# A gated delta rule over 2048 tokens: projections, norms and gates made beside the spike membranes and kept in DRAM, scaled keys moved from GpSimd to VectorE

## What is computed

```python
h = silu(causal_conv(rms(x)))                       # (2048, 128)
q, k, v = heads(h @ Wq), heads(h @ Wk), heads(h @ Wv)   # 8 heads x 64
q = q / (norm(q) + 1e-6);  k = k / (norm(k) + 1e-6)
drive = heads(h @ Wspike)
alpha_base = heads(silu(h @ Wau + bau) @ Wad + bad)
beta_base = h @ Wbeta + bbeta

def step(carry, ins):                               # over 2048 tokens
    s, mem = carry
    mem = 0.9 * mem + dt
    spike = (mem > 0.5)
    mem = mem - spike * 0.5
    alpha = sigmoid(at + asp * spike)
    beta = sigmoid(bt + sum(spike * bsp))
    active = sum(abs(spike)) > 0
    alpha = where(active, alpha, 1);  beta = beta * active
    s = s * alpha
    s = s + (beta * kt) * (vt - kt @ s)
    return (s, mem), qt @ s
```

## Time and profile before

| | us |
|---|---|
| median of 3 runs | 1695.24 (1692.81 to 1695.54) |
| profiled execution, its own time | 1701.06 |
| its span | 1699.3 |
| TensorE busy, weight loads | 1178.4, 902.6 |
| VectorE, ScalarE, GpSimd busy | 1103.5, 601.2, 198.3 |
| mean granted TensorE clock | 0.795 of full |

### The profile page before, as it was taken

One profiled execution on the slowest core, in us unless ns is written; L12 is line 12 of the kernel. 1 busy time (PEld: TensorE's weight loads), 2 busy tenths in 40 slices (PEclk: granted clock), 3 DMA queues, 4 the chain that ended last, 5 costly groups with the idle time before them and its releaser, 6 DMA issues. The chain is left out here.

```text
span 1699.3 us, 25028 instructions
## 1 busy us (share of the span) xinstructions
PE 1178.4 (69%) x8364; PEld 902.6 (53%) x8364; DVE 1103.5 (65%) x3471; ACT 601.2 (35%) x935; POOL 198.3 (12%) x189
## 2 busy tenths in 40 slices
PE   1230001488888988898888988889666879688786
PEld 1110001377777877787777876779423526346272
DVE  4788988777887778877797777872133325343251
ACT  3120000333444334443444534441325355363422
POOL 2000001301211012110211102110010102001000
PEclk8575555688899889898988999895578788886966
DMA  2000000000000000000000000000200000000000
GB/s 72 0 1 1 1 1 1 1 1 0 0 0 0 0 0 0 0 0 0 0 0 0 0 0 0 0 1 1 58 0 1 0 0 8 0 7 1 0 8 6
DMA packets 9746, 7.22 MB, mean 4 GB/s; under 512 B 3158, under 2 KB 7831, under 8 KB 9690
## 3 DMA queue, kind: packets, MB, share of 16 engines
q1 hardware_dynamic: 8170, 5.07, 1.1%
q10 hardware_dynamic: 1520, 1.48, 0.3%
HBM read 5.50 MB, written 1.05 MB: 4 GB/s over the span
## 5 line engine op out<-in xcount | busy, mean ns | idle before, releaser
L1133 DVE TENSOR_TENSOR delta_tm<-delta_tm,ps 128x256 f32<-128x256 f32 x96 | 40.4, 421 | 156.7 <-PE ps L836 156.7
L795 PE MATMUL ps<-delta_kq_up,delta_arena 64*128 64x128 f32 x1024 | 111.2, 400 | 37.2 <-ACT delta_kq L547 36.5
L795 PEld LDWEIGHTS ps<-delta_kq_up,delta_arena 64*128 64x128 f32 x1024 | 102.4, 302 | 62.2 <-ACT delta_kq L547 37.4
L893 PE MATMUL ps<-ones,beta_b 1*128 1x1 f32 x8 | 1.8, 346 | 190.9 <-PEq L339 190.9
L633 ACT ACTIVATE delta_xf<-ps 128x256 f32<-128x256 f32 (+1 forms) x128 | 48.9, 382 | 204.5 <-PE ps L823 140.2
L517 POOL TENSOR_TENSOR delta_km<-delta_beta_k,delta_arena 128x512 f32<-128x512 f32 x16 | 32.6, 2037 | 635.9 <-DVE delta_beta_k L1030 635.9
L834 PE MATMUL ps<-delta_xf,delta_tt 128*128 128x64 f32 x768 | 106.6, 284 | 0.0
L836 PE MATMUL ps<-delta_tt,delta_xf 128*128 128x64 f32 x768 | 106.6, 284 | 0.0
L823 PEld LDWEIGHTS ps<-delta_tm,drive 128*128 128x128 f32 x768 | 95.6, 201 | 17.0 <-DVE delta_zb L984 9.1
L893 PEld LDWEIGHTS ps<-ones,beta_b 1*128 1x128 f32 x8 | 1.8, 322 | 191.1 <-issue 191.1
L823 PE MATMUL ps<-delta_tm,drive 128*128 128x64 f32 x768 | 98.5, 284 | 6.1 <-ACT delta_tm L623 6.1
(11 more groups left out here) (372 smaller groups left out, 2923.1 us busy)
## 6 DMA issues: line engine op xcount, KB each, us to landing
out<-post_rows SPq DMA_DIRECT2D x4, 256.0 KB, 2.3
setup_wmod<-in_L_wmod ACTq DMA_DIRECT2D x2, 384.0 KB, 3.4
post_wff<-in_L_attn_Wff SPq DMA_DIRECT2D x3, 256.0 KB
post_w<-in_L_ffn_w SPq DMA_DIRECT2D x2, 256.0 KB
post_fc_q<-in_L_ffn_fc_q SPq DMA_DIRECT2D x2, 256.0 KB
setup_wspike<-in_L_attn_Wspike ACTq DMA_DIRECT2D x1, 256.0 KB
wq<-in_L_attn_Wq ACTq DMA_DIRECT2D x1, 256.0 KB
wk<-in_L_attn_Wk SPq DMA_DIRECT2D x1, 256.0 KB
```

The source lines that it names most:

```text
L795: ins = eng.matmul(m.ps[:, at + h % 2, P * (h // 2):P * (h // 2) + P], up_lift[s][ks, cs], m.kq_up[s][ks, :, half], start=True, stop=True)
L1133: eng.tensor_tensor(v, v, m.ps[:, 6 + n, 0:256].rearrange("p (b s) -> p b s", s=s), ALU.subtract).then_inc(vector_back, vec.one(f"TX{x}{s}"))
```

## The change

- A function `prepare()` is added to the block of the membranes. In 4 groups of 512 tokens it makes k, q, v, the gate's hidden units (by ScalarE's Silu, with a change of table before and behind), its drive with `wad`, beta's scores from the tokens, sums of squares and norms. TensorE has 7 steps of 4 matmuls of 512 columns in each group, ScalarE 16 to 19 activations, mostly of 128x2048. VectorE multiplies k and q by the inverse norms (`unit`, one 128x2048 multiplication), 8 times in all, put into the membranes' steps 80, 122, 164 and so on. SP stores 5 MB for each group (20 MB in all), and the phase ends when the last store has landed.
- The three passes of the membranes are written out, without the hardware loop. `WARM` is 128, so each pass still has all its 128 steps.
- In `delta_phase` SP loads for each chunk `zb` (512 KB), `kq` (512 KB) and `v` (256 KB). Each load waits until the chunk before has used the tile.
- GpSimd only clears `drive` at the start. Its `km` operations go to VectorE, its product of spikes and their weights becomes four scalar_tensor_tensor that add into `zb`, its squares are gone.
- TensorE loses k, q, v, the hidden units, `wad`, the sums and half of beta's matmuls. The count moves from behind the first join to before `transposed`.
- VectorE loses the hidden units, the guard of the norms and the multiplication by the norms. Each join is split in its halves a and b, with pieces of the front between; the scaled keys are made before `update` where half of `kq_up` was made behind it. ScalarE loses the norms and the copies of k, q, v, and the lifts come earlier.

VectorE's loop, and what TensorE's chunk loses, as a diff:

```diff
             with eng.Fori(0, NT - 1) as i:
                 front_spikes(i + 1)
                 base(i)
-                front_au(i + 1)
                 blocks(i)
                 front_z(i + 1)
                 front_sums(i + 1)
-                join(i, 8)
                 front_active(i + 1)
-                join(i, 16)
-                front_exponents(i + 1)
-                join(i, 32)
-                front_exponents2(i + 1)
+                join(i, 8, "a")
+                join(i, 8, "b")
+                front_decay(i + 1)
+                join(i, 16, "a")
+                front_mid(i + 1)
+                front_splits(i + 1, UPPER[:1])
+                join(i, 16, "b")
+                front_splits(i + 1, UPPER[1:])
+                front_toend(i + 1)
+                join(i, 32, "a")
+                front_beta(i + 1)
+                join(i, 32, "b")
+                front_base(i + 1)
+                front_upper(i + 1, UPPER[:1])
                 rest(i)
-                front_unit(i + 1)
+                front_upper(i + 1, UPPER[1:3])
                 keep(i)
-                front_upper(i + 1, UPPER[:2])
+                front_upper(i + 1, UPPER[3:])
                 update(i)
-                front_upper(i + 1, UPPER[2:])
                 front_late(i + 1)
...
-            def chunk(i, last):
+            def chunk(i):
 
                 base(i)
                 eng.wait_ge(scalar_back, act.before("out", i))
-                front_au(i + 1)
-                blocks(i, True)
-                front_sums(i + 1)
+                blocks(i)
+                front_beta(i + 1)
+                front_count(i + 1)
                 transposed(i)
                 join(i, 8)
-                front_count(i + 1)
                 join(i, 16)
                 join(i, 32)
...
                 last_join(i)
                 state1(i)
                 solve(i)
-                front_late(i + 1)
                 seen_by_q(i)
-                if not last:
-                    eng.wait_ge(scalar_back, act.at("kend", i))
-                    front_k(i + 2)
                 eng.wait_ge(scalar_back, act.at("solved", i))
-                if not last:
-                    front_q(i + 2)
                 state2(i)
```

More of the change, by code:

```diff
@@ L348, in spike_phase, with a_pass @@
         a_half, b_half = slice(0, W), slice(W, 2 * W)
[L349 to L365, removed]
+        unit, n_units = prepare(nc, ctx, m, block)
+        FIRST, EVERY = 80, 42
         @block.vector
         def _(eng):
-            def a_pass():
+            def a_pass(at=None, t0=0):
                 eng.sem_clear(step_a)
@@ L402, in changed @@
                 return value
-            with eng.Fori(0, SURE) as _:
-                a_pass()
+            for n in range(SURE):
+                a_pass(n * P, 0 if n else P - WARM)
             with eng.If(changed() > 0):
@@ L526, in _ @@
             eng.wait_ge(m.chain_v, 2)
-            front(0)
-            with eng.Fori(0, NT - 1) as i:
-                front(i + 1)
         @block.scalar
@@ L713, in head, with front_beta @@
                 return slice(HD * (h % 2), HD * (h % 2) + HD), slice(P * (h // 2), P * (h // 2) + P)
-            def project(bank, w, rhs, rows=P):
+            def front_beta(n):
+                eng.wait_ge(vector_front, fvec.at("spikes", n))
+                eng.wait_ge(vector_back, vec.before("up8b", n))
                 for c in range(NP):
-                    ins = eng.matmul(m.ps[:, bank, c * P:c * P + P], w[:, c * P:c * P + P], rhs, start=True, stop=True)
-                return ins
-            def front_k(n):
-                project(4, m.wk, m.hh[:, tok(n)]).then_inc(tensor_front, fpe.one("k"))
@@ L996, in front_z, with front_decay @@
             def front_z(n):
-                eng.wait_ge(tensor_front, fpe.at("drive_a", n))
-                eng.wait_ge(pool_front, fpool.at("push", n))
-                eng.tensor_tensor(zb[:, 0, :], m.ps[:, 4, :], m.push[:, :, :].rearrange("p c t -> p (c t)"), ALU.add).then_inc(vector_front, fvec.one("z"))
-            def front_exponents(n):
+                eng.wait_ge(zb_in, 16 * n + 16)
+                eng.wait_ge(vector_front, fvec.at("spikes", n))
+                for c in range(NP):
+                    z = zb[:, 0, c * P:c * P + P]
+                    ins = eng.scalar_tensor_tensor(z, m.spk[:, c, :], m.aspike[:, c:c + 1], z, ALU.mult, ALU.add)
+                ins.then_inc(vector_front, fvec.one("z"))
+            def front_decay(n):
                 eng.wait_ge(scalar_front, fact.at("zb_ln", n))
```

431 lines of the change are left out of this document (250 added, 181 removed).

## The result

| | before | changed |
|---|---|---|
| median | 1695.23 us | 1626.53 us, four runs: 1593.62, 1616.52, 1636.54, 1659.90 |
| ratio | | 0.947, 95% interval 0.939 to 0.955 |
| profiled execution, its span | 1701.06, 1699.3 | 1659.90, 1658.2 |
| granted clock | 0.795 | 0.792 |

The change is faster by 69 us where 49 slower was forecast. The ratio rests on the two runs that count as fast, 1593.62 and 1616.52, since a run more than 1.5% above the fastest of its kernel counts as slow; the medians of all four and four runs give 0.959. The runs of one and the same program lie 23, 20 and 23 us apart, where the four of the kernel before lie within 3 (1692.81 to 1695.54). Of 42 more runs of the kernel before, made with the experiments, 40 lie between 1692.78 and 1700.25; two stand out, 1714.28 and 3609.68, and nothing here explains them.

What follows compares the result with a forecast made beforehand. TensorE's stream and its clock, with a few waits between engines, were taken to set the delta loop's step. Membranes +9, ahead of chunk 0 -13, loop -117, lost clock +170 gave +49 us, 1744; 8-in-10 range 1575 to 1860.

Steps and rivals of the forecast that it cites:

- The number of chunks that lose the clock: Delta loop, new TensorE gap ahead of the joins: 8 of 15 chunks lose the clock, between 6 and 11; +170 us.
- the kept step: Delta loop, chunk that keeps the clock: step falls by 7.8 us to 45.6, 117 us over 15 steps.
- What a lost chunk costs: Delta loop, chunk that loses the clock: a step of 66.8 us, 21.2 more than one that keeps it.
- Update to spread: VectorE work in each chunk, 10.1 us: four `kq_up` behind the update and L969 go, -1.9 us.
- solve to update: Each chunk, 8.9 us: L752 and projections ahead of `state2` go, `keep` falls; -4.0 us, between -3 and -4.5.
- Spread to transposes: Each chunk: transposes wait for `tt` and start sooner behind the spread, -0.5 to -1.4 us, taken as -1.0.
- From the transposes to the solve: Joins of each chunk: the count leaves them, -0.9 us.
- Membranes: Membrane phase: eight multiplications +18.3 us, loop turns gone -11.2, last store sticks out 2; sum +9, between +7 and +12.
- Ahead of chunk 0: Before the first spread: hidden units, `wad`, sums, guard, norms and slowing beside GpSimd go; sum -13 us.
- The rule that speaks against: TensorE clock: short gaps keep it and a busy TensorE soon regains it, so nearly nothing would be lost.
- (a): Rival, gap ahead of the joins: clock kept, 3 or fewer chunks lost, 1574 up to 1638 us; chance 0.18.
- (c): Rival: clock lost but the joins bring it back, 3 us per lost chunk, 1598 us; chance 0.05.

Runs made afterwards that it cites:

- the ten runs: The changed kernel's four runs and six more of it unchanged, the six at 1593.85, 1611.10, 1640.59, 1658.51, 1660.96 and 1682.55 us.
- e2_count_back: Changed kernel with the count back behind the first join, and the comparison that reads it behind that join on VectorE: 1708.01 us, 1.011 of before.
- e9_fill_base_too: Changed kernel with useless 128x512 matmuls: two ahead of the count, three ahead of the last chunk's transposes, four ahead of each spread: 1623.00 us, 0.957 of before.
- e3_before_last: Kernel before with three 128x512 matmuls of constants ahead of the last chunk's transposes: 1674.10 us, 0.989 of before.
- e6_proj_place: Changed kernel with two useless matmuls ahead of the count, plus three between the reading by q and the state's second part: 1629.12 us, 0.960 of before.
- e10_wide_early: Changed kernel with the count back behind the first join, plus two 128x512 matmuls of constants right behind the transposes: 1653.53 us, 0.976 of before.
- e7_wide_in_join: Changed kernel with one 128x512 matmul of constants behind the first join: 1607.83 us, 0.946 of before.
- e5_pool_beside: Changed kernel with two useless matmuls ahead of the count, plus five GpSimd multiplications of constants per chunk from beta_k on: 1656.46 us, 0.976 of before.

## Why the prediction was wrong, point by point

- **The number of chunks that lose the clock.** This is the step that failed: "8 of 15 lost, between 6 and 11" against 0 to 4. With 1.8 in place of 8 my own sum gives 1695 + 9 - 13 - 117 + 38 = 1612, where the ten runs' mean is 1635; most of what is left is the kept step below, 15 x 1.3 = 20. The text put the idle time as "some 2.4 us, in one or two pieces" and weighed the total against the earlier trace rows. The runs show that the pieces count: first pieces of 1.2 to 2.1 us with the count behind them kept the clock in the profiled run, those of 2.6 to 2.7 lost it, and 3.6 in one piece always did (e2_count_back). They don't give a rule for when: in e9_fill_base_too pieces of 1.52 and 0.68 us lost it in three steps of fifteen. The estimate of 8 had no row behind it, as the text said, and the sign of the forecast hung on it alone: below 5.7 lost chunks the same sum says faster. That 1626.5 lies in the stated range, 1575 to 1860, is owed to its width; the mechanism forecast, with about half of the chunks lost, is not what happened.
- **What a lost chunk costs.** 21.2 forecast, 22.8 measured. The last chunk's 42 us of joins at half clock were a good preview, and e3_before_last shows that its idle time was the cause. Of the 22.8 us 19 lie between the transposes and the solve (42.7 against 23.7 to 24.2) and 3.8 between the solve and the update.
- **The kept step.** 45.6 forecast, 46.9 measured, which over 15 steps is 20 us. Update to spread 8.3 (8.2 forecast) and solve to update -4.2 (-4.0 forecast) came out in size, but the second for a reason that the text has only in part. It put 3 us on the projections ahead of `state2`. In the kernel before, `state2` was done at 385.65, and the update at 387.09 came behind VectorE's own stream, which ran from 378.84 without a wait that the trace shows:

```profile
384.14 3.03 DVE L1039 TENSOR_TENSOR delta_kq_up<-delta_kq,delta_arena 128x256 f32<-128x256 f32 x4
...
385.02 0.63 PE L888 MATMUL ps<-delta_u_rows,drive 128*64 128x64 f32 x16
```

So both streams had to get shorter: VectorE's lost the multiplication by the norms, moved `kq_base` ahead of `rest` and had 1.1 us less of `keep`; TensorE's lost the projections, and e6_proj_place shows that with VectorE's stream so short they would cost 2.8. What each gave on its own was not tested. Spread to transposes is 10.1, on average only 0.1 less and not 1.0: `tt` ends 9.9 us behind the spread in both kernels, and the last chunk, whose 9.13 I took, has no front beside it on VectorE. From the transposes to the solve 0.4 went on average, not 0.9.
- **Membranes.** +7.1 measured (297.40 against 290.26), +9 forecast. The unrolling gave 11.1, as forecast. The multiplications with their stores cost 18.1, not 20.3: no store stuck out, since the wait between the two phases is 5.6 us in both kernels, and I had put 2 there.
- **Ahead of chunk 0.** From the delta rule's begin to its first spread 37.8 us against 53.5, -15.7; I had -13.
- **The rule that speaks against.** The Trainium skill, TensorE: Matmul & The Clock Gate, section Why this matters for your kernels, would have nearly nothing lost, and so was nearer to the count of lost chunks than I was, though 1.8 of 15 were. That a busy TensorE returns to full clock soon, as its Part 1 has it, the trace contradicts again: a lost chunk stayed at half clock for 43 us of a fully busy TensorE, in each of the three steps.
- **Rivals.** (a) came closest: three or fewer lost in nine of the ten runs, 1574 to 1638 forecast. Its floor is 1593.6 by the measured step, so that three lost are 1662 and five of the ten runs lie above its range. (c), the joins bring it back, came true only in e2_count_back and e10_wide_early, where a wide matmul stood among them.

## What to carry to other kernels

When a change takes work from an engine that wasn't waiting, look at where it now waits, and at what stood in the joins or gaps by chance: a matmul moved forward by one stage can be worth more for the clock it held than for its own microsecond. If runs of one program fall on steps of equal height, count the steps in the trace before averaging them; then fill the one gap with work that nobody reads and see whether the steps go. After each such fill look at the gaps again, since at full clock they are longer.

## What was not expected of the hardware

- TensorE at half clock and busy all the time stayed there through the joins: 43.0 of 43.0 us in the changed kernel, 36.3 of 36.3 in e7_wide_in_join. In the changed kernel's chunk 0 it came back between 396 and 397 us, behind the state's products and with no pause ahead; in e5_pool_beside, behind the same products, after 6.7 us. One 128x512 product among the joins brought the clock back in each of the 15 steps of e2_count_back, and didn't in the one case of e7_wide_in_join, at the same place in the chunk. Why the two differ is open; nothing was run that tells their moment from their operands.
- GpSimd beside VectorE made operations with two inputs from SBUF take 1.4 to 1.5 times as long in e5_pool_beside (681 to 1023, 1218 to 1744 ns), and 1.4 us of added wait from it cost a stretch of 6.7 us at half clock.
- Which chunks lose the clock changes from run to run of the same program. e9_fill_base_too shows fifteen steps with waits alike to 0.01 us and different ends, and its three lost ones lie 252.6 us apart. The Trainium skill, TensorE: Matmul & The Clock Gate, Part 1, says that the chip judges activity in a window that runs freely beside the program, so that the moment matters; the even distance agrees with it, but no run here shifted a gap alone in time, so it stays open.
